# Combining expert outputs on three engines: blocks handed from VectorE to ScalarE and TensorE, and the kept tail from GpSimd to them

## The chip, the cores and the metric

The kernel runs on one core of a Trainium2 chip. The metric is device time in microseconds (us) of one execution; lower is better. A core has four engines that compute, each with its own in-order instruction queue: TensorE (PE, matrix products into PSUM), VectorE (DVE), ScalarE (ACT) and GpSimd (POOL); SyncE (SP) issues most transfers. They meet only through semaphores. PSUM has eight banks of 128 x 512 words.

## What is computed

Two layers over 8192 nodes of width 128. The first is a graph convolution over 32 graphs. The second, which the change touches, is a mixture of four experts whose gates come from an attention layer over 524,288 edges:

```python
agg = segment_sum(h[src] * alpha, dst) + b_gat
scores = layernorm(agg).reshape(M, HEADS, NUM_EXPERTS).mean(1)
topk_s, topk_i = top_k(scores, 2);  w = softmax(topk_s)
for ei in range(4):
    g = where(topk_i == ei, w, 0).sum(-1)
    out = out + g[..., None] * (gelu(x @ W1[ei] + b1[ei]) @ W2[ei] + b2[ei])
x = x + out
```

Everything is fp32; `out` is one sum per node of four gated expert outputs and the residual `x`.

## The kernel before

The nodes are 64 tiles of 128 (`xs[:, t, :]`), two tiles to a group. The expert outputs of all nodes (512 words per node) are computed early, before the gates are known. Those of 24 groups (48 tiles) are stored to HBM and those of the last 8 groups (16 tiles, `eo_kept`) stay on the chip. A **block** is two groups, four tiles; there are 12 stored blocks, 0 to 11, and four kept ones.

The end of the kernel, from about 885 us, goes in four **parts** of 16 tiles, `g` = 0 to 3. Before it, and beside it, GpSimd gathers one table row per edge list entry with 384 indirect transfers (L554), 96 for each part; part `g` can begin when `rows_in[g]` is complete. In each part:

- ScalarE regroups the gathered rows (L950), TensorE transposes them (L784), VectorE computes attention weights (`weights`, L1438 to L1450), which TensorE transposes back (L789) and ScalarE puts in place (L942).
- VectorE multiplies (`values`, L1457); ScalarE and VectorE split the rows into three bf16 pieces (L932, L1464, L937, L1469).
- TensorE sums over the edges, 48 products into four banks of `ps_H`, then 48 into four banks of `ps_four` (L797). VectorE empties each half (`take_bank`, L1478). ScalarE moves half of the result across partitions by a transfer (L963), and TensorE and ScalarE prepare the marks of the next part (`mark`, L773 and L924 to L927).
- VectorE merges and computes the gates (`merge`, `gating`, L1487 to L1561) with one Exp on ScalarE in between (L970).

`combine(b)` (L1577) adds the four gated expert outputs of block `b` to `xs` on VectorE, 16 instructions of 128 x 128. A block is loaded from HBM by SP (L462, 1 MB) into one of four slots, which come free when the slot's earlier block is combined (`SLOT_OF`), and stored by SP when `combined` says so (L487). The order on VectorE is written by hand: the blocks of a part's nodes are combined during the next part, two before `take_bank` and two after it; in part 3 two of them stand before `weights` instead. So blocks 0 to 3 fall in part 1, blocks 4 to 7 in part 2 and blocks 8 to 11 in part 3, together with the kernel's last gates.

After the last gates come the 16 kept tiles: VectorE combines eight of them as above, ScalarE scales the other eight (L976), and GpSimd adds their four pieces and the residual (L592, L594, L596). SP stores them, and the kernel ends.

Of the kernel before, what the change touches and what calls it, by code (L numbers as in the profile page):

```python
# [24 lines left out]
GRAPHS, NODES, D = 32, 256, 128  # L25
# [10 lines left out]
OWN = M // P  # L36
# [28 lines left out]
PART_BLOCKS = BLOCKS // (PARTS - 1)  # L65
SLOT_OF = (0, 1, 0, 1, 0, 1, 2, 0, 1, 2, 3, 0)
KEPT_BLOCKS = 2

def build(nc, x, adj, eps, W1, b1, rms_w, W2, b2, W_gat, att_src, att_dst, b_gat, ln_g, ln_b,  # L70
# [4 lines left out]
    with ctx:  # L75
# [44 lines left out]
        def region(at):  # L120

            def take(shape, dt=fp32):
# [9 lines left out]
                if len(shape) > 1:  # L132
# [173 lines left out]
        sums = [ps_H[:, :, :, :].rearrange("p a b n -> p (a b n)").rearrange("p (g w) -> p g w", g=4), ps_four[:, :, :]]  # L306
# [17 lines left out]
                 "combined", "others_combined", "sum_chain", "gated", "iota_done", "zero_done"]  # L324
# [63 lines left out]

        def part_tiles(m, g):

            return m[:, g * PART_TILES:(g + 1) * PART_TILES]

        others = [(eo_kept[:, t, :], TILES - PAIR * KEPT + t) for t in range(KEPT_BLOCKS * BLOCK_TILES, PAIR * KEPT)]
# [4 lines left out]
        def _(sp):  # L398
# [100 lines left out]
            for b in range(KEPT_BLOCKS):  # L499
                sp.wait_ge(s["combined"], BLOCKS + b + 1)  # L500
                rstore(GROUPS - KEPT + BLOCK * b, BLOCK, out_stored[1])
            for b in range(KEPT // BLOCK - KEPT_BLOCKS):
                sp.wait_ge(s["others_combined"], BLOCK_TILES * (b + 1))
                rstore(GROUPS - KEPT + BLOCK * (KEPT_BLOCKS + b), BLOCK, out_stored[0])
            sp.wait_ge(out_stored[0], 16 * (KEPT // BLOCK - KEPT_BLOCKS))
            sp.wait_ge(out_stored[1], 16 * (BLOCKS + KEPT_BLOCKS))
# [5 lines left out]
        def _(pool):  # L512
# [73 lines left out]

            pool.wait_ge(s["gates_ready"], PARTS)
            for n, (of, t) in enumerate(others):
                row = xs[:, t, :]  # L590
                pool.wait_ge(s["gated"], n + 1)
                pool.tensor_tensor(of[:, 0:2 * D], of[:, 0:2 * D], of[:, 2 * D:4 * D], ALU.add).then_inc(s["sum_chain"], 1)  # L592
                pool.wait_ge(s["sum_chain"], 2 * n + 1)
                pool.tensor_tensor(of[:, 0:D], of[:, 0:D], of[:, D:2 * D], ALU.add).then_inc(s["sum_chain"], 1)  # L594
                pool.wait_ge(s["sum_chain"], 2 * n + 2)
                pool.tensor_tensor(row, row, of[:, 0:D], ALU.add).then_inc(s["others_combined"], 1)  # L596

        @block.tensor
        def _(pe):
# [167 lines left out]
            def mark(g):  # L767

                if g:
                    pe.wait_ge(s["agg_out"], 2 * g - 1)  # L770
                    pe.wait_ge(s["marks_ready"], g)
                for k, m in enumerate((self_, empty)):
                    last = nc.tensor.matmul(halfH[2 + k][:, 0:OWNED], chosen[:, g, :], m, start=True, stop=True)  # L773
                last.then_inc(s["marks_in_psum"], 1)

            pe.wait_ge(s["marks_made"], 1)
            mark(0)
            for g in range(PARTS):
                if g:
                    pe.wait_ge(s["agg_out"], 2 * g)  # L780
                for k in range(2):
# [3 lines left out]
                    last.then_inc(s["terms_in_psum"], 1)  # L785
                for k, ready in ((1, "back_ready"), (0, "exp_done")):
# [14 lines left out]
                if g + 1 < PARTS:  # L801
                    mark(g + 1)

        @block.scalar
        def _(act):
# [114 lines left out]
            def mark(g):  # L920
# [3 lines left out]
                nc.scalar.activation(marks[:, 0, 0:OWNED], halfH[2][:, 0:OWNED], ACT.Identity)  # L924
                nc.scalar.activation(marks[:, 1, 0:OWNED], halfH[2][:, 0:OWNED], ACT.Identity, bias=ones[:, 0:1], scale=-1.0)
# [706 lines left out]
```

## Time and profile before

| what | value |
|---|---|
| time, median of 3 runs | 1152.58 us (1148.36 to 1153.88) |
| the profiled execution | 1152.78 us, its span 1151.0 us |
| VectorE busy | 905.2 us, 79% of the span |
| TensorE busy, mean granted clock | 802.5 us, 0.769 of full speed |
| ScalarE, GpSimd busy | 440.0 us, 611.7 us |
| the stage that the change touches | about 885 us to the end |

How to read it: all rows come from one profiled execution, in microseconds from the start of its span.
### The profile page before, as it was taken

The numbers are of one execution on the slowest core, as the hardware profiler recorded it, in microseconds if no ns is written. First come the engines' busy times: TensorE is split into PE (matmuls) and PEld (weight loads), VectorE is DVE, ScalarE is ACT, GpSimd is POOL, SyncE is SP. The second block draws the span as 40 slices with busy tenths as digits, with TensorE's granted clock in tenths as the row PEclk, the third lists the DMA queues.
The fourth block names the chain that finished last, engine by engine and source line by source line (L and its number), as shares of the span: only waits on it lengthen the run. The fifth ranks groups of instructions, "written<-read, shape, count | busy, mean of one in ns | idle before, by whom it ended". The sixth has DMA issues, their size and how long they took to land. (4 is left out here: it accounts for less than half of the span.)

```text
span 1151.0 us, 17715 instructions
## 1 busy us (share of the span) xinstructions
PE 802.5 (70%) x5180; PEld 688.4 (60%) x5180; DVE 905.2 (79%) x3070; ACT 440.0 (38%) x1069; POOL 611.7 (53%) x553
## 2 busy tenths in 40 slices
PE   0004888989999988969999999999996415041130
PEld 0003777878888977848888888888884404040030
DVE  7999787867888877997999501888887578989877
ACT  1008788884455544525555553000001212120303
POOL 2000000006777760077777777888887778888004
PEclk9999888888999988979999999555555555555555
DMA  8000011112222112112222300000000012425001
GB/s 251 2 0 28 24 32 43 31 44 48 56 48 63 30 9 27 74 47 65 83 65 83 100 10 9 7 6 7 6 7 9 10 49 82 156 59 178 19 22 37
DMA packets 73043, 55.45 MB, mean 48 GB/s; under 512 B 32534, under 2 KB 65689, under 8 KB 72988
## 3 DMA queue, kind: packets, MB, share of 16 engines
q1 hardware_dynamic: 56140, 48.72, 13.4%
q0 software_dynamic: 16384, 5.54, 5.3%
q10 hardware_dynamic: 464, 0.59, 0.2%
q8 instruction: 19, 0.31, 0.1%
q14 instruction: 36, 0.29, 0.1%
HBM read 36.65 MB, written 17.76 MB: 47 GB/s over the span
## 5 line engine op out<-in xcount | busy, mean ns | idle before, releaser
L554 POOL DMA_INDIRECT sb_arena<-table,sb_arena x384 | 463.7, 1208 | 169.5 <-issue 116.7
L538 POOL DMA_INDIRECT sb_late<-lists,sb_window_at x128 | 127.9, 999 | 297.6 <-DMA lists<-sb_arena 255.9
L729 PE MATMUL ps_four<-sb_late 128*128 128x64 bf16 x1232 | 159.8, 301 | 3.7 <-DVE sb_late L1307 0.3
L1305 DVE TENSOR_TENSOR sb_late<-sb_far_lo,sb_iota_lo 128x1792 bf16<-128x1792 bf16 x88 | 96.1, 1092 | 84.0 <-PE ps_four L729 81.0
L729 PEld LDWEIGHTS ps_four<-sb_late 128*128 128x128 bf16 x1232 | 141.8, 143 | 21.5 <-DVE sb_late L1307 18.3
L702 PE MATMUL ps_four<-sb_we,sb_arena 128*128 128x128 f32 x1024 | 131.9, 282 | 0.0
L702 PEld LDWEIGHTS ps_four<-sb_we,sb_arena 128*128 128x128 f32 x1024 | 119.7, 192 | 14.7 <-issue 14.7
L694 PE MATMUL ps_H<-sb_x2nT,sb_we 128*128 (+1 forms) x512 | 124.7, 388 | 0.0
L887 ACT ACTIVATE sb_arena<-ps_H,sb_be_c 128x256 f32<-128x256 f32 x256 | 107.0, 470 | 30.7 <-PE ps_H L694 28.7
L694 PEld LDWEIGHTS ps_H<-sb_x2nT,sb_we 128*128 128x128 f32 x512 | 95.2, 196 | 11.0
L820 ACT ACTIVATE sb_arena<-sb_arena,sb_owner_mid 128x368 f32<-128x368 f32 x128 | 76.8, 600 | 53.4 <-DVE sb_arena L1048 49.8
L636 PE MATMUL ps_four<-sb_arena 128*128 128x256 f32 x128 | 37.0, 415 | 73.4 <-DVE sb_var L1162 73.4
L628 PE MATMUL ps_H<-sb_arena,sb_w 128*128 128x256 f32 x256 | 82.9, 481 | 0.2 <-DVE sb_arena L1229 0.2
L671 PE MATMUL ps_four<-sb_ones,sb_arena 128*128 128x1 f32 x512 | 65.9, 258 | 16.3 <-ACT sb_arena L838 16.3
L671 PEld LDWEIGHTS ps_four<-sb_ones,sb_arena 128*128 128x128 f32 x512 | 66.0, 209 | 18.1 <-ACT sb_arena L833 18.1
L636 PEld LDWEIGHTS ps_four<-sb_arena 128*128 128x128 f32 x128 | 27.5, 221 | 80.3 <-DVE sb_arena L1216 74.1
L1229 DVE SCALAR_TENSOR_TENSOR sb_arena<-ps_H,sb_b_c,sb_arena 128x256 f32<-128x256 f32 x128 | 53.1, 477 | 23.8 <-ACT sb_arena L843 23.2
L647 PE MATMUL ps_four<-sb_w,sb_arena 128*128 128x128 f32 x512 | 69.0, 291 | 0.0
L854 ACT ACTIVATE sb_arena<-sb_arena,sb_rms_c 128x256 f32<-128x256 f32 x128 | 54.6, 497 | 37.4 <-DVE sb_arena L1229 37.4
L924 ACT ACT_TABLE_LOAD x1 | 1.3, 1283 | 170.6 <-PE ps_H L773 170.6
L628 PEld LDWEIGHTS ps_H<-sb_arena,sb_w 128*128 128x128 f32 x256 | 59.1, 242 | 10.1 <-issue 0.5
L647 PEld LDWEIGHTS ps_four<-sb_w,sb_arena 128*128 128x128 f32 x512 | 62.7, 200 | 3.9 <-issue 0.2
(247 smaller groups left out, 1422.5 us busy)
## 6 DMA issues: line engine op xcount, KB each, us to landing
outputs<-sb_arena SPq DMA_DIRECT2D x24, 512.0 KB, 2.7
sb_arena<-outputs SPq DMA_DIRECT2D x12, 1024.0 KB, 6.3
sb_arena<-in_adj SPq DMA_DIRECT2D x32, 256.0 KB
sb_arena<-table,sb_arena POOLq DMA_INDIRECT x384, 2.8
sb_x2nT<-in_L_ffn_edge_index SPq DMA_DIRECT2D x8, 512.0 KB, 7.6
sb_xs<-in_x SPq DMA_DIRECT2D x32, 128.0 KB, 2.2
out_x<-sb_xs SPq DMA_DIRECT2D x16, 256.0 KB, 2.6
sb_late<-lists,sb_window_at POOLq DMA_INDIRECT x128
```

The source lines that it names most:

```text
L538: pool.indirect_dma_start(bk.bitcast(i32)[:, p * WINDOW:(p + 1) * WINDOW], None, lists, bass.IndirectOffsetOnAxis(ap=window_at[:, p:p + 1] ...
L554: pool.indirect_dma_start(rows[:, g, c, o, :], None, table[0:M, :], bass.IndirectOffsetOnAxis(ap=idxT[:, at:at + 1], axis=0), bounds_check ...
L628: last = nc.tensor.matmul(ps_H[:, q, c, :], w1[:, c * P:(c + 1) * P], aggT[:, q, :], start=True, stop=True)
L636: last = nc.tensor.matmul(ps_A, xn[:, p, mt, :], adjT[:, p, mt, :], start=(mt == 0), stop=(mt == 1))
L647: last = nc.tensor.matmul(ps_O[:, nt, :], ss[:, q, c, nt * P:(nt + 1) * P], w2[:, c, :], start=False, stop=(nt == 1 and c == HC - 1))
L671: last = nc.tensor.matmul(ps_Q[:, u:u + 1], sq[:, q, c, u * P:(u + 1) * P], ones[:, 0:1], start=(c == 0), stop=(c == HC - 1))
L694: last = nc.tensor.matmul(halfH[e][:, c * GROUP:(c + 1) * GROUP], we1[:, e, c * P:(c + 1) * P], x2nT[:, bass.ds(g * GROUP, GROUP)], start= ...
L702: last = nc.tensor.matmul(obank[k][:, (j // 2) * D:(j // 2 + 1) * D], hh[1 - p][:, j, k * P:(k + 1) * P], we2[:, j, :], start=False, stop= ...
L729: last = nc.tensor.matmul(ps_F, hot_lo[k][:, :, c], hot_hi[k][:, :, c], start=(first and c == 0), stop=(end and c == FB - 1))
L820: nc.scalar.activation(sign_out, owner, ACT.Sign, bias=owner_mid[:, o:o + 1], scale=2.0, accum_out=above[:, o:o + 1]).then_inc(s["above_co ...
L887: last = nc.scalar.activation(hh[p][:, 2 * e + c, :], halfH[e][:, c * GROUP:(c + 1) * GROUP], ACT.Gelu, bias=be1_c[:, 2 * e + c:2 * e + c ...
L1305: V.tensor_tensor(hot_lo[k], far_lo[:, bass.ds(b * FB, FB)].unsqueeze(1).to_broadcast([P, P, FB]), iota_lo[:, :, :], ALU.is_equal)
```

## The change

- **Between parts.** Of the 12 stored blocks six (2, 3, 6, 7, 8, 9: `SUMMED`) leave VectorE's `combine`. For each of them ScalarE multiplies the 16 pieces by their gates in place (`scale_block`), TensorE adds the four experts of the block's four tiles by four products with the identity into one bank (`block_sum`), and VectorE adds that bank to `xs` in one instruction (`add_sum`). Blocks 0, 1, 4, 5, 10 and 11 stay on VectorE, now one before the two `take_bank` and one after. Blocks 8 and 9 move from VectorE to this path, ahead of `weights` of part 3, and so does block 7, which stood in part 2.
- **Banks.** The edge sums use three banks of each half in place of four, with six batches to a bank, so that two banks are free for `block_sum`; `take_bank` reads each half with four instructions in place of two. The marks move to other banks, so that `mark` waits for both halves to be emptied, where it waited for one.
- **The end.** VectorE combines ten kept tiles in place of eight. For the other six ScalarE scales, TensorE adds the four pieces and the residual into a bank, and ScalarE copies the sum to `xs`. GpSimd has no work there. The kept tiles are stored by eight transfers of one group in place of four of two.

The diff at its core:

```diff
+PER_BANK = 6
-KEPT_BLOCKS = 2
+KEPT_TILES = 10
-        sums = [ps_H[:, :, :, :].rearrange("p a b n -> p (a b n)").rearrange("p (g w) -> p g w", g=4), ps_four[:, :, :]]
+        sums = [ps_H[:, :, :, :].rearrange("p a b n -> p (a b n)").rearrange("p (g w) -> p g w", g=4)[:, 0:3, :], ps_four[:, 0:3, :]]
+        marks_bank = [halfH[2], bank_O[:, :]]
+        block_bank = [bank_S[:, :], halfH[3]]
+        SUMMED = (2, 3, 6, 7, 8, 9)
...
 @block.gpsimd
-            for n, (of, t) in enumerate(others):
-                pool.tensor_tensor(of[:, 0:2 * D], of[:, 0:2 * D], of[:, 2 * D:4 * D], ALU.add)
-                pool.tensor_tensor(of[:, 0:D], of[:, 0:D], of[:, D:2 * D], ALU.add)
-                pool.tensor_tensor(row, row, of[:, 0:D], ALU.add)
...
 @block.tensor
             def mark(g):
-                    pe.wait_ge(s["agg_out"], 2 * g - 1)
+                    pe.wait_ge(s["agg_out"], 2 * g)
+            def block_sum(b):
+                pe.wait_ge(s["scaled"], SUMMED.index(b) + 1)
+                some(pe, s["combined"], b - 1, None)
+                of = eo_back[SLOT_OF[b]]
+                for e in range(EXPERTS):
+                    last = nc.tensor.matmul(block_bank[b % 2], ident[:, :], of[:, :, e * D:(e + 1) * D],
+                                            start=(e == 0), stop=(e == EXPERTS - 1))
+                last.then_inc(s["block_in_psum"], 1)
             for g in range(PARTS):
+                if g == PARTS - 1:
+                    for b in (block_of(g - 1, 3), block_of(g, 0), block_of(g, 1)):
+                        block_sum(b)
...
+                if g == 2:
+                    block_sum(block_of(g - 1, 3))
...
+                if g in (1, 2):
+                    block_sum(block_of(g, 2))
+            for n, (of, t) in enumerate(others):
+                pe.wait_ge(s["gated"], n + 1)
+                for e in range(EXPERTS):
+                    nc.tensor.matmul(others_bank[n], ident[:, :], of[:, e * D:(e + 1) * D], start=(e == 0), stop=False)
+                nc.tensor.matmul(others_bank[n], ident[:, :], xs[:, t, :], start=False, stop=True)
...
 @block.scalar
+            def scale_block(b):
+                act.wait_ge(s["gates_ready"], b // PART_BLOCKS + 1)
+                act.wait_ge(eo_loaded[SLOT_OF[b]], 16 * turns(b))
+                for u in range(BLOCK_TILES):
+                    for e in range(EXPERTS):
+                        last = nc.scalar.activation(of, of, ACT.Identity, scale=gates[:, b * BLOCK_TILES + u, e:e + 1])
+                last.then_inc(s["scaled"], 1)
             for g in range(PARTS):
+                if g == PARTS - 1:
+                    for b in (block_of(g - 1, 3), block_of(g, 0), block_of(g, 1)):
+                        scale_block(b)
+                by_heads(g)
+                if g == 2:
+                    scale_block(block_of(g - 1, 3))
...
+                if g in (1, 2):
+                    scale_block(block_of(g, 2))
+            gate(0)
+            gate(1)
+            for n in range(2, len(others)):
+                gate(n)
+                keep_sum(n - 2)
...
 @block.vector
+            def add_sum(b):
+                dve.wait_ge(s["block_in_psum"], SUMMED.index(b) + 1)
+                V.tensor_tensor(to, to, block_bank[b % 2].rearrange("p (t d) -> p t d", t=BLOCK_TILES), ALU.add)
             for g in range(PARTS):
                 if g == PARTS - 1:
-                    combine(before.pop(0))
-                    combine(before.pop(0))
+                    for b in (block_of(g - 1, 3), block_of(g, 0), block_of(g, 1)):
+                        add_sum(b)
...
-                for b in before[:len(before) // 2]:
-                    combine(b)
+                if g == 2:
+                    add_sum(block_of(g - 1, 3))
+                if g:
+                    combine(block_of(g, 0 if g < PARTS - 1 else 2))
                 take_bank(2 * g)
                 take_bank(2 * g + 1)
-                for b in before[len(before) // 2:]:
-                    combine(b)
+                if g:
+                    combine(block_of(g, 1 if g < PARTS - 1 else 3))
                 merge(g)
                 gating(g)
+                if g in (1, 2):
+                    add_sum(block_of(g, 2))
-            for b in range(KEPT_BLOCKS):
-                combine(BLOCKS + b)
+            combine_kept(0, 4)
+            combine_kept(4, 4)
+            combine_kept(8, KEPT_TILES - 8)
```

Here `block_of(g, k)` is block `4 (g - 1) + k`. The order of the instructions shows it at two engines. The first place is ScalarE between the merge of part 2 and the Exp of part 3's weights; before, with `rows_in3` the gathers of part 3:

```order
L967 ACTIVATE sb_late<-sb_late 128x16x4 [waits merge_in]
L968 ACTIVATE sb_far_e<-sb_far_e 128x64
L970 ACTIVATE sb_gates<-sb_sc 128x64 [waits gates_e]
L950 ACTIVATE sb_iota_lo<-sb_arena 128x384 [waits terms_in_psum,rows_in3]
L950 ACTIVATE sb_iota_lo<-sb_arena 128x384 [waits terms_in_psum]
L953 ACTIVATE sb_arena<-sb_arena 128x384 [waits exp_in]
```

and after, where L976 is the scaling of a block, L984 the regrouping and L1015 the gates' Exp (`eo_loaded2` is the load into slot 2):

```order
L1011 ACTIVATE sb_far_e<-sb_far_e 128x64
L976 ACTIVATE sb_arena<-sb_arena,sb_gates 128x128 [waits eo_loaded2,gates_ready]
L976 ACTIVATE sb_arena<-sb_arena,sb_gates 128x128 x15
L1015 ACTIVATE sb_gates<-sb_sc 128x64 [waits gates_e]
L976 ACTIVATE sb_arena<-sb_arena,sb_gates 128x128 [waits eo_loaded0,gates_ready]
L976 ACTIVATE sb_arena<-sb_arena,sb_gates 128x128 x15
L976 ACTIVATE sb_arena<-sb_arena,sb_gates 128x128 [waits eo_loaded1,gates_ready]
L976 ACTIVATE sb_arena<-sb_arena,sb_gates 128x128 x15
L976 ACTIVATE sb_arena<-sb_arena,sb_gates 128x128 [waits eo_loaded2,gates_ready]
L976 ACTIVATE sb_arena<-sb_arena,sb_gates 128x128 x15
L984 ACTIVATE sb_iota_lo<-sb_arena 128x384 [waits terms_in_psum,rows_in3]
```

Four scalings moved in, of blocks 6, 7, 8 and 9, and three of them stand ahead of the regrouping of part 3. The second place is TensorE between the edge sums of part 2 and the first transposes of part 3; before:

```order
L797 MATMUL ps_four<-sb_late,sb_arena 64x72 x47
L773 MATMUL ps_H<-sb_arena,sb_epsI 128x384 [waits marks_ready,agg_out]
L773 MATMUL ps_H<-sb_arena,sb_epsI 128x384
L784 MATMUL ps_H<-sb_ident,sb_iota_lo 128x128 [waits by_head_ready,agg_out]
L784 MATMUL ps_H<-sb_ident,sb_iota_lo 128x128 x2
```

and after, where L782 is `block_sum` and L797 the transposes of the terms:

```order
L773 MATMUL ps_H<-sb_arena,sb_epsI 128x384 [waits marks_ready,agg_out]
L773 MATMUL ps_four<-sb_arena,sb_epsI 128x384
L782 MATMUL ps_four<-sb_arena,sb_ident 128x512 [waits combined,scaled]
L782 MATMUL ps_four<-sb_arena,sb_ident 128x512 x3
L782 MATMUL ps_H<-sb_arena,sb_ident 128x512 [waits combined,scaled]
L782 MATMUL ps_H<-sb_arena,sb_ident 128x512 x3
L782 MATMUL ps_four<-sb_arena,sb_ident 128x512 [waits combined,scaled]
L782 MATMUL ps_four<-sb_arena,sb_ident 128x512 x3
L782 MATMUL ps_H<-sb_arena,sb_ident 128x512 [waits combined,scaled]
L782 MATMUL ps_H<-sb_arena,sb_ident 128x512 x3
L797 MATMUL ps_H<-sb_ident,sb_iota_lo 128x128 [waits by_head_ready,agg_out]
```

Four sums of four products each moved in, and the transposes of part 3 now stand behind them.

## Rows read from the trace of the kernel before

**Rows 1.** The page: busy time of the engines, granted clock in 40 slices.

```profile
PE 802.5 (70%) x5180; PEld 688.4 (60%) x5180; DVE 905.2 (79%) x3070; ACT 440.0 (38%) x1069; POOL 611.7 (53%) x553
PEclk9999888888999988979999999555555555555555
```

**Rows 2.** Chain that ended last: start us, us, what.

```profile
1127.02 15.47 DVE sb_xs L1577 x29
```

**Rows 3.** Timeline of VectorE, part 0, which combines no block.

```profile
906.65 2.64 DVE L1469 TENSOR_TENSOR sb_late<-sb_arena,sb_late 128x1152 bf16<-128x1152 f32 x2
914.14 1.42 DVE L1478 TENSOR_REDUCE sb_late<-ps_H 64x192 f32<-64x576 f32 x2 [4.86 <-PE ps_H L797]
919.90 1.41 DVE L1478 TENSOR_REDUCE sb_late<-ps_four 64x192 f32<-64x576 f32 x2 [4.34 <-PE ps_four L797]
925.56 0.23 DVE L1487 TENSOR_TENSOR sb_a_dst<-sb_late,sb_far_e 128x64 f32<-128x64 f32 x1 [4.25 <-DMA sb_late<-sb_late]
```

**Rows 4.** Timeline of VectorE, part 1: first block combined, start of the merge.

```profile
965.23 8.48 DVE L1577 SCALAR_TENSOR_TENSOR sb_xs<-sb_arena,sb_gates,sb_xs 128x128 f32<-128x128 f32 x32
...
986.26 0.22 DVE L1487 TENSOR_TENSOR sb_a_dst<-sb_late,sb_far_e 128x64 f32<-128x64 f32 x1
```

**Rows 5.** Timeline of VectorE, part 2, then two blocks and the weights of part 3.

```profile
1025.81 8.48 DVE L1577 SCALAR_TENSOR_TENSOR sb_xs<-sb_arena,sb_gates,sb_xs 128x128 f32<-128x128 f32 x32
...
1046.24 0.21 DVE L1487 TENSOR_TENSOR sb_a_dst<-sb_late,sb_far_e 128x64 f32<-128x64 f32 x1
...
1066.67 8.48 DVE L1577 SCALAR_TENSOR_TENSOR sb_xs<-sb_arena,sb_gates,sb_xs 128x128 f32<-128x128 f32 x32
1075.07 0.54 DVE L1438 TENSOR_TENSOR sb_arena<-ps_H,sb_arena 128x384 f32<-128x384 f32 x1
```

**Rows 6.** Timeline of ScalarE: gates' Exp of parts 1 and 2, regrouping, kept scaling.

```profile
1001.72 0.26 ACT L970 ACTIVATE sb_gates<-sb_sc 128x64 f32<-128x64 f32 x1 [14.41 <-DVE sb_sc L1556]
...
1061.70 0.26 ACT L970 ACTIVATE sb_gates<-sb_sc 128x64 f32<-128x64 f32 x1 [14.42 <-DVE sb_sc L1556]
1068.13 2.21 ACT L950 ACTIVATE sb_iota_lo<-sb_arena 128x384 f32<-128x384 f32 x2 [6.17 <-DMA sb_arena<-table,sb_arena]
...
1127.02 9.45 ACT L976 ACTIVATE sb_x2nT<-sb_x2nT,sb_gates 128x128 f32<-128x128 f32 x32 [1.09 <-DVE sb_gates L1561]
```

**Rows 7.** Timeline of TensorE: transposes back, marks, transposes of the terms.

```profile
1014.37 1.54 PE L789 MATMUL ps_four<-sb_ident,sb_arena 128*128 128x128 f32 x6 [9.34 <-DVE sb_arena L1450]
...
1036.40 2.93 PE L773 MATMUL ps_H<-sb_arena,sb_epsI 128*128 128x384 f32 x4
1069.44 1.86 PE L784 MATMUL ps_H<-sb_ident,sb_iota_lo 128*128 128x128 f32 x6 [30.11 <-ACT sb_iota_lo L950]
```

**Rows 8.** Stretches: us, busy PE, PEld, DVE, ACT, POOL, granted clock, DMA share, GB/s.

```profile
1025.00:1035.00 10.00, 10.00 (x86) 10.00 (x85) 10.00 (x35) 0.00 (x0) 8.78 (x5) 0.50 0.45 132
...
1040.00:1041.00 1.00, 0.00 (x0) 0.00 (x0) 1.00 (x6) 1.00 (x3) 1.00 (x1) 1.00 0.69 189
```

**Rows 9.** The page, groups of TensorE at the high clock: count | busy us, mean ns.

```profile
L702 PE MATMUL ps_four<-sb_we,sb_arena 128*128 128x128 f32 x1024 | 131.9, 282 | 0.0
L694 PE MATMUL ps_H<-sb_x2nT,sb_we 128*128 (+1 forms) x512 | 124.7, 388 | 0.0
```

**Rows 10.** Stretches of the end, all engines, columns as in rows 8.

```profile
1127.00:1128.40 1.40, 0.00 (x0) 0.00 (x0) 1.38 (x6) 1.38 (x5) 0.00 (x0) 0.50 0.00 0
1128.50:1136.50 8.00, 0.00 (x0) 0.00 (x0) 8.00 (x14) 7.97 (x28) 7.31 (x13) 0.50 0.09 28
1136.50:1142.90 6.40, 0.00 (x0) 0.00 (x0) 6.40 (x12) 0.00 (x0) 5.81 (x11) 0.50 0.03 8
```

**Rows 11.** Line 487, the stores of `out_x`: duration ns, first and last start.

```profile
L487 SPq DMA_DIRECT2D out_x<-sb_xs x16: 380/386/551, 969.5 to 1144.5; - x16
```

**Rows 12.** Line 1438, a 128 x 384 add from PSUM: duration ns min/median/max.

```profile
L1438 DVE TENSOR_TENSOR sb_arena<-ps_H,sb_arena x4: 543/547/557, 889.5 to 1075.1; 128x384 f32<-128x384 f32 x4
```

**Rows 13.** Line 462, the block loads of 1 MB, issue to landing.

```profile
DMA to landing us min/median/max: 5.0/6.3/9.5
```

More of the change, by code:

```diff
@@ L1473, in take_bank @@
                 dve.wait_ge(s["agg_in_psum"], k + 1)
-                by_part = sums[k % 2][0:OWN, :, 0:4 * 3 * ROW].rearrange("p g (t u s v) -> p g t u s v", u=2, s=3, v=ROW)
-                tiles_ = slice(BATCH // 2 * (k % 2), BATCH // 2 * (k % 2 + 1))
-                outs = [m[k // 2 % 2][0:OWN, tiles_, :].rearrange("p (g t) v -> p g t v", g=4) for m in (agg, odd)]
-                for u, o in enumerate(outs):
-                    last = V.reduce_sum(o, by_part[:, :, :, u, :, :].rearrange("p g t s v -> p g t v s"), AX.X)
+                for first, past, each in ((0, 2, PER_BANK), (2, 3, BATCH - 2 * PER_BANK)):
+                    by_bank = sums[k % 2][0:OWN, first:past, 0:each * 3 * ROW].rearrange("p g (t u s v) -> p g t u s v", u=2, s=3, v=ROW)
+                    at = BATCH // 2 * (k % 2) + first * PER_BANK // 2
+                    for u, m in enumerate((agg, odd)):
+                        o = m[k // 2 % 2][0:OWN, at:at + (past - first) * each // 2, :].rearrange("p (g t) v -> p g t v", g=past - first)
+                        last = V.reduce_sum(o, by_bank[:, :, :, u, :, :].rearrange("p g t s v -> p g t v s"), AX.X)
                 last.then_inc(s["agg_out"], 1)
@@ L1581, in combine @@
                 last.then_inc(s["combined"], 1)
+                gated_n[0] += (EXPERTS - 1) * BLOCK_TILES
             for g in range(PARTS):
-                before = [PART_BLOCKS * (g - 1) + b for b in range(PART_BLOCKS)] if g else []
                 hots_of(2 * g)
@@ L1595, in _, with combine_kept @@
                 lowest(2 * g + 1)
[L1596 to L1597 removed]
+                if g == 2:
+                    add_sum(block_of(g - 1, 3))
+                if g:
+                    combine(block_of(g, 0 if g < PARTS - 1 else 2))
                 take_bank(2 * g)
                 take_bank(2 * g + 1)
[L1600 to L1601 removed]
+                if g:
+                    combine(block_of(g, 1 if g < PARTS - 1 else 3))
                 merge(g)
                 gating(g)
[L1604 to L1605 removed]
+                if g in (1, 2):
+                    add_sum(block_of(g, 2))
+            def combine_kept(first, n):
+                base = gated_n[0] + (EXPERTS - 1) * first
+                for e in range(EXPERTS):
+                    for u in range(n):
+                        row = xs[:, TILES - PAIR * KEPT + first + u, :]
+                        if e:
+                            dve.wait_ge(s["comb_chain"], base + (e - 1) * n + u + 1)
+                        last = V.scalar_tensor_tensor(row, eo_kept[:, first + u, e * D:(e + 1) * D],
+                                                      gates[:, TILES - PAIR * KEPT + first + u, e:e + 1], row, ALU.mult, ALU.add)
+                        if e < EXPERTS - 1:
+                            last.then_inc(s["comb_chain"], 1)
+                        elif u % PAIR:
+                            last.then_inc(s["combined"], 1)
+            combine_kept(0, 4)
+            combine_kept(4, 4)
+            combine_kept(8, KEPT_TILES - 8)
 _INS = ["x", "adj", "L0_gnn_epsilon", "L0_gnn_W1", "L0_gnn_b1", "L0_gnn_rms_weight", "L0_gnn_W2", "L0_gnn_b2",
```

74 lines of the change are left out of this document (40 added, 34 removed).

## The prediction

> **What bounds the kernel now.** I read the page first. VectorE has the largest busy share, 79%, but TensorE is at 70% and its clock is at the low level in the whole last part of the span [rows 1], so an average decides nothing and the end has to be read as a stage of its own. The chain that ended last gives its final piece: VectorE combining kept tiles from 1127.02 on [rows 2]. From there I went back along VectorE's timeline.
>
> In part 0, which has no block to combine, VectorE waits three times between its last remainder (906.65 + 2.64 = 909.3) and the merge at 925.56: 4.86 and 4.34 us for the two halves of the edge sums and 4.25 us for a transfer, 16.3 us in all [rows 3]. In parts 1 and 2 it combines four blocks there. A block costs 8.48 / 2 = 4.24 us, so four cost 17.0 us, and the same stretch takes 986.26 - 965.23 = 21.0 us and 1046.24 - 1025.81 = 20.4 us [rows 4, 5]. So of 17.0 us of combining only 4 to 5 us stand on the path; the rest fills waits that part 0 shows empty. VectorE bounds parts 1 and 2, by little.
>
> Part 3 has a second bound. Its regrouping on ScalarE began at 1068.13, after 6.17 us of waiting for the gathers [rows 6], and the transposes at 1069.44 for 1.86 us [rows 7], so the terms were there at 1071.3; VectorE reached the weights at 1075.07, after two blocks [rows 5]. A lead that VectorE wins in parts 1 and 2 is worth at most 1075.1 - 1071.3 = 3.8 us if the gathers stay where they are.
>
> In the tail the same combining runs at half speed. Six instructions ran in the first 1.38 us, beside ScalarE alone: 0.23 to 0.27 us each. Beside GpSimd there were 14 in 8.00 us and, with ScalarE done, 12 in 6.40 us: 0.53 to 0.57 each [rows 10]. So GpSimd's adds slow it, not ScalarE.
>
> **The change, part by part.** The sum is made against the profiled execution, 1152.78 us, whose span is 1151.0 us with 1.8 us around it; that is 0.2 us above the median of the runs shown, 1152.58.
>
> *Emptying the edge sums.* Four instructions in place of two move the same words. Two more starts cost between 0 and 0.4 us: an instruction over 576 words takes 1.42 / 2 = 0.71 us [rows 3], one over 384 takes 0.55 [rows 12], so the fixed part is at most about 0.2. I take +0.2 us per half. The first half's share lies beside TensorE's second half (5.8 us from one to the other, 919.90 - 914.14); the second's is on the path, in each of four parts.
>
> *The marks* now wait for both halves. They are needed only before the merge's Exp, and the 2.93 us of TensorE [rows 7] and four short copies lie beside the transfer's 4.25 us [rows 3]. I cost them at nothing; without that cover it would be up to 0.5 us in each of three parts.
>
> *Parts 1 and 2 on VectorE.* One block (4.24) goes into the first wait (4.86) and one into the transfer's (4.25), so the stretch falls to part 0's 16.3 + 0.2 = 16.5 us. Part 1 wins 21.0 - 16.5 = 4.5. Each `add_sum` adds 512 words from PSUM: by the 0.55 us for 384, 0.7 us [rows 12]. Block 2's is added after part 1's gates, +0.7. Block 3's stands before a combine in part 2: 0.7 + 4.24 = 4.9 against the wait of 4.86, so +0.1; part 2 wins 20.4 - 16.6 = 3.8. With +0.2 from part 0 the Exp of part 2's gates ends 0.2 - 4.5 + 0.7 - 3.8 = -7.4 us earlier, at 1061.96 - 7.4 = 1054.6 [rows 6].
>
> *What a block costs TensorE.* Four products of 512 columns, eight matrix instructions. Low clock: six transposes of 128 columns take 1.54 us [rows 7], about 0.22 each, so eight of 512 cost 8 x 4 x 0.22 = 7.2 us; the marks' four of 384 columns in 2.93 us give 7.8 at most. I take 7.3. High clock: 512 instructions of 256 columns in 124.7 us are 0.244 each [rows 9], so eight of 512 cost at most 3.9 us. Which one? The clock stood at 0.50 through ten us of edge sums that kept TensorE busy all the time, and was at 1.00 in the microsecond after the marks' four fp32 products [rows 7, 8]. A block's sum is eight such fp32 instructions, so I let it rise inside the first sum of a row: 5.6 us, the middle of 3.9 and 7.3, and 3.9 for those that follow at once.
>
> *Block 3's sum* stands between two transposes that part 2 needs. It can start 2.2 us (regrouping) plus one scaling after the gates' Exp of part 1. A scaling is 16 instructions: 9.45 / 32 x 16 = 4.7 us [rows 6]. So it runs from 6.9 to 12.5 us after the Exp (14.2 at the low clock). The transposes back wait for VectorE until 1014.37 - 1001.98 = 12.4 us after it [rows 6, 7], 13.1 with block 2's add. Cost 0, bound +1.1. Blocks 2 and 6 are scaled and summed beside `gating` (ScalarE waits 14.4 us there [rows 6]); they cost nothing.
>
> *Part 3 up to the weights.* Three scalings now stand ahead of the regrouping on ScalarE's queue: 1054.6 + 0.1 + 3 x 4.7 = 1068.8. The load for block 9 needs slot 2, free only when block 6 is added: gates at 1054.6 + 1.1 [rows 6], the add at 1056.4, a store and the load issued by 1057.3, landed 5.0 to 9.5, median 6.3 us later [rows 13]: 1063.6, in time for its scaling at 1064.1, at worst 2.7 us late. TensorE sums block 7 from 1059.4 to 1065.0, block 8 to 1068.9, block 9 to 1072.8. Behind that wait the transposes of part 3, and on VectorE the three adds ahead of the weights. VectorE starts the weights at 1072.8 + 0.7 and a step, 1073.6. Before: 1075.07. That is -1.5 us, and VectorE's lead of 7.4 us is spent waiting. The gathers, even unchanged at 1068.1, are no longer last.
>
> *Part 3 after the weights* is as before, +0.2 for the second half.
>
> *The tail.* VectorE: 40 instructions at 0.265 are 10.6 us. The path over TensorE: the first tile scaled at 1.3 us, ten instructions a tile, 0.22 each low, 131.9 / 1024 = 0.129 each high [rows 9]. Two tiles low (to 5.7) and four high (1.3 each) end at 10.9, the copy and steps at 11.6. All low: 1.3 + 6 x 2.2 + 0.5 = 15.0; all high it is ScalarE's 24 scalings and six copies, about 9 to 11. SP then issues the last VectorE store and three more, 0.39 us each [rows 11] and 0.45 with the step between: the last begins at 10.6 + 3 x 0.45 + 0.1 = 12.1 us after the gates. Before, it began at 1144.5 - 1127.0 = 17.5 [rows 11]. That is -5.4 us, bounds -6 and -2.4. What follows the last store I leave as it was.
>
> Sum: -1.5 + 0.2 - 5.4 = -6.7, so 1152.78 - 6.7 = **1146.1 us**.
>
> **A page on the clock.** The Trainium skill, TensorE: Matmul & The Clock Gate (HAM oscillation), says that a TensorE left waiting falls to half rate and that each burst after a wait starts there. This speaks against the change, which puts short bursts into waits. By it alone blocks 2, 3, 6, 7 and the tail begin low, as I have them; if none of them rose again, the result would be the first rival's. The trace agrees on the fall: 0.50 in most of the end, and 1.00 only for some microseconds after the marks [rows 1, 8].
>
> **Rivals.** (1) *TensorE becomes the bound.* The clock stays at 0.50. Three sums then cost 3 x 7.3 = 21.9 from 1059.4: 1081.3, the weights at 1082.1, +7.0; the tail -2.4 at best: 1152.8 + 7.0 + 0.2 - 2.4 = 1157.6, slower than before. It decides from 5.0 us a sum (1059.4 + 3 x 5.0 + 0.8 = 1075.2). For it: 0.50 in every slice of the end [rows 1]. Against: the rise after the marks. (2) *Only the tail's products stay low*, after 15 us in which TensorE has nothing to do: -1.5 + 0.2 - 2.4 = -3.7, 1149.1. (3) *The load of block 9 is late* by 2.7: 1148.8. For it: it is issued beside the last gathers and a store; against: the median. (4) *The change does not free VectorE*: the kept tiles run slowly for another reason. Then 40 x 0.53 = 21.2 us, the tail +5.1, 1156.6. Rows 10 speak against it. (5) *VectorE's lead arrives*, if ScalarE and TensorE are done sooner than their rows say: the weights at 1071.3, -3.8 in place of -1.5: 1143.8.
>
> **How the numbers follow.** Forecast 0.62; rivals 0.10, 0.12, 0.07, 0.03 and 0.06. The forecast's own range is 1143.5 to 1149.5: costs of +1.7 (block 7 wholly low), +1.1 (block 3) and 1.5 (marks) one way, less than my 3.9 and 0.2 the other, and executions of before that differ by 5.5 us. Half a percent, 5.8 us, is about what a measurement of this kernel can tell from no change; faster means below 1146.8, slower above 1158.3. A little over half of the forecast, and rival 5, are below: 0.44. Slower: half of rival 1, some of 4 and what I have not seen: 0.10. The rest, 0.46, lies between. The range 1142.5 to 1154 leaves out rivals 1 and 4 and little else.
>
> **What would show it.** Right: the weights of part 3 released by TensorE and not by a combine, at 1073 to 1075; the granted clock at 1.00 during the sums of blocks 8 and 9; the kept combines at 0.265 us each; no idle time over 1 us at `add_sum` of block 3. Wrong: sums of 7 us each, a scaling of block 9 that waits for its load, or a last store more than 13 us after the gates.

## The result: 0.9913 of the time before, and the profile after

The changed kernel took 1141.27 us, median of 6 runs (1136.81 to 1142.21), beside 1149.96 us (6 runs) for the kernel before; the ratio is 0.9913, 95% interval 0.989 to 0.9937. A second comparison on one chip (the first run of the experiments) gave 0.9888, 0.9872 to 0.9904. The profiled execution took 1141.60 us with a span of 1139.9 us, 11.1 us less than the span before. The prediction had 6.7 us less, 1146.1, with 1142.5 as the low end of its range: the direction is right, and for the profiled execution the forecast gain is 4.5 us too small. In medians the gain is 8.7 us (12.2 in the second comparison). The forecast started from an execution of 1152.78 us, 2.8 us above the median of the six, so a part of the distance to its range is scatter of the kernel before.

To see where the 11.1 us are, the span is best cut at two instructions that stand in both kernels: VectorE's reciprocal in the gating of part 0 and in that of part 3. They are shown for the kernel before, then for the kernel after (timeline of VectorE: start us, duration us, what).

```profile
941.89 0.25 DVE L1560 RECIPROCAL sb_gs<-sb_gs 128x16 f32<-128x16 f32 x1
...
1126.47 0.25 DVE L1560 RECIPROCAL sb_gs<-sb_gs 128x16 f32<-128x16 f32 x1
```

```profile
942.83 0.25 DVE L1619 RECIPROCAL sb_gs<-sb_gs 128x16 f32<-128x16 f32 x1
...
1124.84 0.25 DVE L1619 RECIPROCAL sb_gs<-sb_gs 128x16 f32<-128x16 f32 x1
```

| kernel | to part 0 | parts 0 to 3 | part 3 to the end | span |
|---|---|---|---|---|
| before | 941.9 | 184.6 | 24.5 | 1151.0 |
| after | 942.8 | 182.0 | 15.1 | 1139.9 |
| changed again | 943.8 | 182.8 | 15.0 | 1141.6 |
| one late GpSimd add | 942.6 | 182.7 | 20.0 | 1145.3 |
| the same add, early | 939.4 | 182.8 | 15.2 | 1137.4 |
| stores in pairs | 942.5 | 182.6 | 15.1 | 1140.2 |
| new end alone | 939.5 | 184.6 | 15.0 | 1139.1 |
| new work between parts alone | 943.0 | 182.5 | 24.6 | 1150.1 |
| regrouping first | 941.4 | 171.4 | 15.0 | 1127.8 |
| three blocks on VectorE | 943.7 | 179.2 | 15.0 | 1137.9 |
| one-hot rows early | 941.8 | 174.6 | 15.1 | 1131.4 |

The first column is nearly the same work in all of them and still differs by 4.4 us from run to run; the six times of the changed kernel differ by 5.4. The other two repeat within 0.8 and 0.2 us wherever the code is the same. So the gain is 1.8 to 2.6 us between the parts and 9.5 us behind the last gates.

**Between the parts** VectorE's timeline answers to [rows 3 to 5]. These rows are parts 1 and 2 of after; the bracket is the idle time ahead and what ended it.

```profile
966.17 4.28 DVE L1641 SCALAR_TENSOR_TENSOR sb_xs<-sb_arena,sb_gates,sb_xs 128x128 f32<-128x128 f32 x16
971.10 1.54 DVE L1537 TENSOR_REDUCE sb_late<-ps_H 64x144 f32<-64x432 f32 x4 [0.66 <-PE ps_H L812]
976.86 1.54 DVE L1537 TENSOR_REDUCE sb_late<-ps_four 64x144 f32<-64x432 f32 x4 [4.22 <-PE ps_four L812]
978.33 4.27 DVE L1641 SCALAR_TENSOR_TENSOR sb_xs<-sb_arena,sb_gates,sb_xs 128x128 f32<-128x128 f32 x16
...
1039.08 0.23 DVE L1546 TENSOR_TENSOR sb_a_dst<-sb_late,sb_far_e 128x64 f32<-128x64 f32 x1 [0.27 <-DMA sb_late<-sb_late]
```

One block fills the wait for the first half of the edge sums to 0.66 us, the other that for the transfer to 0.27 us or nothing. The wait for the second half, 4.22 us, stays empty. In part 3 the three adds come ahead of the weights:

```profile
1065.83 0.69 DVE L1627 TENSOR_TENSOR sb_xs<-sb_xs,ps_H 128x512 f32<-128x512 f32 x1 [5.70 <-PE ps_H L782]
1069.27 0.69 DVE L1627 TENSOR_TENSOR sb_xs<-sb_xs,ps_four 128x512 f32<-128x512 f32 x1 [2.75 <-PE ps_four L782]
1072.70 0.69 DVE L1627 TENSOR_TENSOR sb_xs<-sb_xs,ps_H 128x512 f32<-128x512 f32 x1 [2.75 <-PE ps_H L782]
1073.31 0.55 DVE L1496 TENSOR_TENSOR sb_arena<-ps_H,sb_arena 128x384 f32<-128x384 f32 x1
```

VectorE stands idle for 5.70 + 2.75 + 2.75 = 11.2 us and then starts the weights, 1.8 us sooner than the kernel before [rows 5]. What it waits for is on TensorE, and TensorE's first sum on ScalarE:

```profile
1054.65 14.11 ACT L976 ACTIVATE sb_arena<-sb_arena,sb_gates 128x128 f32<-128x128 f32 x48
1068.67 2.19 ACT L984 ACTIVATE sb_iota_lo<-sb_arena 128x384 f32<-128x384 f32 x2
```

```profile
1059.47 6.33 PE L782 MATMUL ps_H<-sb_arena,sb_ident 128*128 128x512 f32 x8 [9.51 <-ACT sb_arena L976]
1065.63 3.60 PE L782 MATMUL ps_four<-sb_arena,sb_ident 128*128 128x512 f32 x8
1069.07 3.60 PE L782 MATMUL ps_H<-sb_arena,sb_ident 128*128 128x512 f32 x8
1072.50 0.82 PE L797 MATMUL ps_H<-sb_ident,sb_iota_lo 128*128 128x128 f32 x6
```

The clock of these sums is in the stretches (columns as in [rows 8]): 0.50 at the start of block 7's sum, after 9.5 us of waiting, and full from block 8's on.

```profile
1059.50:1062.50 3.00, 3.00 (x4) 1.45 (x5) 0.63 (x2) 3.00 (x11) 0.00 (x0) 0.50 0.68 261
1062.50:1065.50 3.00, 3.00 (x5) 1.11 (x5) 0.00 (x0) 3.00 (x12) 0.00 (x0) 0.62 0.00 0
1065.70:1072.40 6.70, 6.70 (x17) 2.92 (x16) 1.37 (x2) 5.16 (x13) 0.00 (x0) 1.00 0.74 239
```

**At the end** 40 combines of kept tiles start at 1125.38 and take 10.59 us, 0.265 each; beside GpSimd they took 0.53 to 0.57 [rows 10]. The last store starts at 1137.5, 12.1 us after the gates; before it was 17.5 [rows 11]. That is 5.4 us. The timeline of VectorE, then the stores' line as in [rows 11]:

```profile
1125.38 10.59 DVE L1681 SCALAR_TENSOR_TENSOR sb_xs<-sb_x2nT,sb_gates,sb_xs 128x128 f32<-128x128 f32 x40
```

```profile
L498 SPq DMA_DIRECT2D out_x<-sb_xs x20: 380/386/513, 970.5 to 1137.5; - x20
```

The rest lies behind the last store, in the closing instructions of the program's end. GpSimd's last add in the kernel before, then line 75 of that kernel (engine's queue, operation, count: duration ns min/median/max, start us), then line 76 of after:

```profile
1142.42 0.45 POOL L596 TENSOR_TENSOR sb_xs<-sb_xs,sb_x2nT 128x128 f32<-128x128 f32 x1
```

```profile
L75 POOLq DRAIN  x1: 8424/8424/8424, 1142.4 to 1142.4; - x1
L75 SPq COMPARE_BRANCH  x1: 38/38/38, 1147.8 to 1147.8; - x1
L75 SPq EVENT_SEMAPHORE  x1: 17/17/17, 1151.0 to 1151.0; - x1
```

```profile
L76 POOLq DRAIN  x1: 26904/26904/26904, 1035.6 to 1035.6; - x1
L76 SPq COMPARE_BRANCH  x1: 38/38/38, 1139.5 to 1139.5; - x1
L76 SPq EVENT_SEMAPHORE  x1: 17/17/17, 1139.8 to 1139.8; - x1
```

SyncE's branch stands behind its wait for the last store. Before, it came at 1147.8, and nothing closed until GpSimd's drain was over at 1142.4 + 8.4 = 1150.8, 8.0 us after the end of its last add (1142.42 + 0.45). After, the drain stands in GpSimd's queue from 1035.6 and is over at 1062.5, 7.9 us after the end of its last gather instruction:

```profile
1053.64 1.00 POOL L565 DMA_INDIRECT sb_arena<-table,sb_arena  x1 [0.30 <-issue]
```

With that long past, the span closes 0.4 us after SyncE. Behind the last store there were 6.5 us before and 2.4 after: 3.2 against 0.4 from SyncE's branch on, and 3.3 against 2.0 from the store to the branch.

### The profile page after: what moved, and what is told of

The parts are those of the page before. It is cut to its first block and busy times, and to the rows that moved or that the text cites. A ratio compares the mean times of both kernels' runs of the same rounds, so it can differ in the third digit from the quotient of the medians.

```text
span 1139.9 us, 17951 instructions
## 1 busy us (share of the span) xinstructions
PE 840.0 (74%) x5288; PEld 708.7 (62%) x5288; DVE 879.0 (77%) x3004; ACT 466.9 (41%) x1163; POOL 585.8 (51%) x529
## 5 line engine op out<-in xcount | busy, mean ns | idle before, releaser
L565 POOL DMA_INDIRECT sb_arena<-table,sb_arena x384 | 451.0, 1174 | 169.5 <-issue 116.7
L671 PEld LDWEIGHTS ps_four<-sb_ones,sb_arena 128*128 128x128 f32 x512 | 66.5, 210 | 17.5 <-ACT sb_arena L857 17.4
```

The costliest lines, as they stand in the source:

```text
L565: pool.indirect_dma_start(rows[:, g, c, o, :], None, table[0:M, :], bass.IndirectOffsetOnAxis(ap=idxT[:, at:at + 1], axis=0), bounds_check ...
L671: last = nc.tensor.matmul(ps_Q[:, u:u + 1], sq[:, q, c, u * P:(u + 1) * P], ones[:, 0:1], start=(c == 0), stop=(c == HC - 1))
```

## Experiments

The theory: the mechanisms of the prediction hold and GpSimd's drain is the part that it missed. The first rival: the smaller stores (128 KB in place of 256) give the gain at the end. The second: it lies between the parts. Four kernels went on one chip first.

**The changed kernel again.**

> The changed kernel as it is, on the same chip as the three kernels below, as their base. Profiled span near 1139.9 us, last store starting near 1137.6, GpSimd's closing drain over long before. All theories expect the same here.

Measured: 1140.75 us, ratio 0.9888 (0.9872 to 0.9904). The span is 1141.6, 1.7 above the expectation, 1.8 us of it lying ahead of part 3's gates; behind them it is 15.0 us, as in the first profile (15.1).

**One late GpSimd add.**

```
+            pool.wait_ge(s["others_in_psum"], len(others))
+            pool.tensor_tensor(masked[:, 0, :], ident[:, :], ident[:, :], ALU.add)
```

> One GpSimd add of 128x128 on scratch is put behind TensorE's last sum (about 1134.4 us); nothing waits for it. Theory (GpSimd's closing drain, which lasted 8.4 us in the kernel before, held its end): the add ends near 1135.0, the drain about 8.0 later near 1143.0, the span near 1143.3, 3.4 us longer than the changed kernel's; SyncE is past its waits near 1139.5 as without it. Rival (the gain at the end came from the smaller stores): span 1139.9, no change. Rival (any GpSimd instruction costs its own length): +0.5 at most.

Measured: 1145.66 us, ratio 0.9935 (0.9918 to 0.9952), 4.9 us above the changed kernel on the same chip. Its timeline of GpSimd and its closing instructions:

```profile
1136.72 0.40 POOL L599 TENSOR_TENSOR sb_late<-sb_ident 128x128 f32<-128x128 f32 x1 [82.17 <-PE ps_H L829]
```

```profile
L76 POOLq DRAIN  x1: 8361/8361/8361, 1136.7 to 1136.7; - x1
L76 SPq COMPARE_BRANCH  x1: 38/38/38, 1140.0 to 1140.0; - x1
```

An add of 0.40 us whose result nobody reads costs 4.9 us. SyncE is done when it was, and the span (1145.3) closes 0.2 us after the drain (1136.7 + 8.4 = 1145.1). The size is above the expected 3.4 because TensorE's last sum, and so the add, came 2.3 us later than I had put it.

**The same add at the gates.**

```
+            pool.wait_ge(s["gates_ready"], PARTS)
+            pool.tensor_tensor(masked[:, 0, :], ident[:, :], ident[:, :], ALU.add)
```

> The same GpSimd add, but as soon as the last part's gates are there (about 1125.4 us). Theory (drain): the drain ends near 1134, 5 us before the last store has landed, so the span stays at 1139.9 within 0.4. Rival (a GpSimd instruction anywhere near the end costs): near 1143, as the late one. Rival (the stores): 1139.9.

Measured: 1140.18 us, ratio 0.9885 (0.9863 to 0.9907), as the changed kernel.

```profile
L76 POOLq DRAIN  x1: 8517/8517/8517, 1122.8 to 1122.8; - x1
L76 SPq COMPARE_BRANCH  x1: 37/37/37, 1137.0 to 1137.0; - x1
```

The drain is as long (8.5 us), ends at 1131.3, before the last store, and costs nothing: 15.2 us from the gates to the end. So it is not the instruction that costs but how late it is: in both the drain is over 7.9 us after the end of the add. The rival of the smaller stores said no change for both adds; the late one refutes it as the whole cause.

**Stores of 256 KB.**

```
-            for g in range(KEPT_TILES // PAIR):
+            for g, n in ((0, 2), (2, 2), (4, 1)):
...
-            for g in range(KEPT - KEPT_TILES // PAIR):
+            for g, n in ((0, 1), (1, 2)):
```

> The kept tiles are stored in transfers of 256 KB (two groups) where there are two, so that the last one is of 256 KB, as in the kernel before. Theory (drain for most of it, store size for the rest): the last store starts where it did and lands 1.0 us later (2.9 against 1.9 us), span near 1140.9, +1.0. Rival (store size is the whole gain at the end): +4.2, span near 1144.

Measured: 1141.28 us, ratio 0.9899 (0.9882 to 0.9915), no change; 15.1 us behind the gates. Part of my expectation was wrong: five stores in place of eight leave SyncE sooner (its last issue ends 12.1 us after the start of the kept combines, in place of 12.6), and the larger one lands about 0.4 later, so nothing is left. Storing in fewer, larger pieces costs nothing in the end. What differs in the kernel before is how much is stored at the very end. Its last three stores, of 256 KB each, were issued within 1.5 us:

```profile
1143.57 0.93 SPq L487 DMA_DIRECT2D out_x<-sb_xs  x2
...
1144.00 1.10 SPq L487 DMA_DIRECT2D out_x<-sb_xs  x2
```

(two stretches of the timeline that overlap in the store at 1144.00). From the start of the last store to SyncE's branch it took 3.3 us there. In this run the last three stores hold 0.52 MB in place of 0.79, issued within 1.4 us, and it took 2.4; in the changed kernel 0.39 MB within 1.6 us, and 2.0. I read the 1.3 us as that volume; no run put all of it back with the rest of the new end, so smaller stores stay a possible cause of this part.

**The two halves of the change, each alone**, in a second comparison on one chip. The new end with the work between the parts of before:

```
-KEPT_BLOCKS = 2
+KEPT_TILES = 10
...
+                nc.tensor.matmul(others_bank[n], ident[:, :], xs[:, t, :], start=False, stop=True).then_inc(s["others_in_psum"], 1)
...
-                pool.tensor_tensor(row, row, of[:, 0:D], ALU.add).then_inc(s["others_combined"], 1)
```

> The kernel before with the new end alone (VectorE ten kept tiles, ScalarE and TensorE six, no GpSimd); the work between parts is as before. Theory (the end is worth 24.0 - 14.5 us from the last part's gates to the end of the span, the work between parts 1.6): gates near 1127.0, span 1141.5, 9.5 less than before, ratio 0.992. Rival (the gain lies between the parts, the end only uncovers it): ratio above 0.996.

Measured: 1140.31 us, ratio 0.9897 (0.9869 to 0.9926). Parts 0 to 3 take 184.6 us, as before, and the end 15.0, as after; that the span is 2.4 below the expectation lies ahead of part 0's gates (939.5 against 941.9).

The changed work between the parts with the end of before (the same hunks the other way round):

> The changed work between parts with the old end (VectorE eight kept tiles, ScalarE eight, GpSimd adds them). Theory: gates near 1125.4, the span 24.0 later near 1149.4, 1.6 less than before (ratio 0.9986); GpSimd's last add ends some 16 us after the gates, and its closing drain about 8.0 us later is the last thing in the span, 3 us after SyncE has passed its waits. Rival (the gain lies between the parts): ratio under 0.995. Rival (the drain is not what holds the end): the drain ends before SyncE's last wait.

Measured: 1150.83 us, ratio 0.9968 (0.9946 to 0.9989). Parts 0 to 3 take 182.5, the end 24.6, and the drain holds it again:

```profile
L76 POOLq DRAIN  x1: 8424/8424/8424, 1141.4 to 1141.4; - x1
L76 SPq COMPARE_BRANCH  x1: 38/38/38, 1146.8 to 1146.8; - x1
```

1141.4 + 8.4 = 1149.8 of 1150.1. The two halves add up to the whole change (9.5 and 2.1 us of the cut spans), and the rival that puts the gain between the parts falls: its ratios were above 0.996 for the first kernel and under 0.995 for the second. (The second interval just reaches 0.995; the cut spans decide.)

**Regrouping first.** If the 11.2 us that VectorE waits in part 3 are the price of the order, another order has them back. ScalarE scales one block only ahead of the regrouping, TensorE transposes ahead of its sums, and VectorE starts the weights at once. Block 9 goes back to VectorE, so that block 10 falls into the empty wait for the second half.

```
-        SUMMED = (2, 3, 6, 7, 8, 9)
+        SUMMED = (2, 3, 6, 7, 8)
...
                 if g == PARTS - 1:
-                    for b in (block_of(g - 1, 3), block_of(g, 0), block_of(g, 1)):
-                        scale_block(b)
+                    scale_block(block_of(g - 1, 3))
                 by_heads(g)
...
+                if g == PARTS - 1:
+                    scale_block(block_of(g, 0))
...
                 take_bank(2 * g)
+                if g == PARTS - 1:
+                    combine(block_of(g, 2))
                 take_bank(2 * g + 1)
```

> The changed kernel, but in the last part ScalarE regroups the gathered rows behind one scaled block instead of three, TensorE transposes them ahead of its block sums, VectorE starts the weights at once, adds the two sums in later waits and takes the third block itself while it waits for the second bank. Theory (the 11.2 us that VectorE waits for three block sums are the price of the order; the gathers have landed by 1059.4): weights start near 1062.6 instead of 1073.3, gates near 1114.9, span near 1129.4, 10.5 under the changed kernel's; if the gathers land as late as 1062.5, weights near 1065.7 and span 1132.5. Rival (the gathers bind, as in the kernel before, where they were regrouped at 1068.1): weights near 1071, span near 1137.5. Rival (TensorE's block sums at the low clock, 6.3 us each, now delay the transposes back and the bank sums): 3 to 6 us of the gain are given back, span 1133 to 1136.

Measured: 1128.91 us (1125.73 to 1131.34), ratio 0.9788 (0.9762 to 0.9815): the fastest kernel of all, some 12 us under the changed one. Timelines of ScalarE, then of TensorE, then of VectorE:

```profile
1058.87 2.19 ACT L983 ACTIVATE sb_iota_lo<-sb_arena 128x384 f32<-128x384 f32 x2
```

```profile
1060.16 1.86 PE L794 MATMUL ps_H<-sb_ident,sb_iota_lo 128*128 128x128 f32 x6 [9.74 <-ACT sb_iota_lo L983]
1061.81 5.87 PE L782 MATMUL ps_H<-sb_arena,sb_ident 128*128 128x512 f32 x8
```

```profile
1061.17 0.56 DVE L1496 TENSOR_TENSOR sb_arena<-ps_H,sb_arena 128x384 f32<-128x384 f32 x1 [1.48 <-PE ps_H L794]
```

The regrouping follows the scaling without a wait, so the gathers had landed by 1058.9, and the weights start at 1061.17, 12.1 us sooner than in after; expected were 1062.6. Neither rival came: the gathers do not bind at 1068, where the kernel before still waited for them [rows 6], and block 7's sum, at 0.50 until 1066, ends at 1067.7, before VectorE adds it at 1069.14. Parts 0 to 3 are 171.4 us against 182.0 to 182.8. From the start of the weights to the reciprocal of part 3 it takes 51.6 us against 51.5, so the whole gain lies ahead of the weights; handing block 9 back was not tried without the new order.

**Three blocks on VectorE in the middle parts too**, which takes two of the five sums away (the cut is shown against the kernel with the regrouping first).

```
-        SUMMED = (2, 3, 6, 7, 8)
+        SUMMED = (3, 7, 8)
...
-                if g == PARTS - 1:
-                    combine(block_of(g, 2))
+                if g:
+                    combine(block_of(g, 1 if g < PARTS - 1 else 2))
```

> The same, and in the two middle parts VectorE combines a third block itself, while it waits for the second bank (4.22 us), so that two of the five block sums go. Theory (the 4.28 us of a block fit this wait, and the two adds of 0.69 us go): span 1.4 under that of the kernel with the regrouping moved, near 1128.0. Rival (the third block of the first of these parts, loaded only when the first one is done, has not landed): VectorE waits up to 2 us for it there, span 0.6 above.

Measured: 1137.86 us, ratio 0.9864 (0.9837 to 0.9891), 9 us slower than the last one; 7.8 us of it lie between the gates of parts 0 and 3. Theory and rival both missed. From gates to gates part 1 takes 58.1 us (56.0 with the regrouping alone) and part 2 takes 63.2 (57.5): the worst waits are in part 2, not in part 1.

```profile
1035.00 4.29 DVE L1637 SCALAR_TENSOR_TENSOR sb_xs<-sb_arena,sb_gates,sb_xs 128x128 f32<-128x128 f32 x16 [2.90 <-DMA sb_arena<-outputs]
1040.67 4.27 DVE L1637 SCALAR_TENSOR_TENSOR sb_xs<-sb_arena,sb_gates,sb_xs 128x128 f32<-128x128 f32 x16
1048.52 0.23 DVE L1542 TENSOR_TENSOR sb_a_dst<-sb_late,sb_far_e 128x64 f32<-128x64 f32 x1 [3.58 <-DMA sb_late<-sb_late]
```

Block 5 is combined one wait sooner and its load has not landed (2.90 us), and behind that the transfer of the odd rows is late (3.58, against 0.98 with the order of the last kernel).

**One-hot rows early.** The same wait filled without a third block: VectorE's second block between the two halves, the next part's one-hot rows in the transfer's wait (the cut is shown against the changed kernel).

```
-                hots_of(2 * g)
-                hots_of(2 * g + 1)
...
+                if g:
+                    combine(block_of(g, 1 if g < PARTS - 1 else 2))
                 take_bank(2 * g + 1)
+                if g < PARTS - 1:
+                    hots_of(2 * g + 2)
+                    hots_of(2 * g + 3)
+                else:
+                    combine(block_of(g, 3))
```

> The kernel with the regrouping moved, and besides in every part VectorE's second block goes into the wait for the second bank (4.22 us) and the one-hot rows of the next part (3.69 us) into the wait for the transfer of the odd rows (4.3 to 4.5 us); loads are as they were. From part to part VectorE gains 3.6 to 3.7 us, so the third part's gates come some 10.5 us sooner after those of part 0 (102.9 instead of 113.4). Theory (the gathers of the last part now bind: the last one is issued near 1053 and lands some 2.9 us later): ScalarE waits for them, the weights of part 3 start near 1059.3 instead of 1061.2, span near 1126.0, 1.9 less. Rival (VectorE binds to the end): the gain of three parts arrives, span near 1117. Rival (earlier loads and sums collide with the odd rows' transfer, as with the third block on VectorE): gain under 5 us in the parts, span 1128 or above.

Measured (another chip): 1133.09 us, ratio 0.9837 (0.9819 to 0.9854), slower than with the regrouping alone. The theory's gathers do not bind; in part 2 the rival of the collisions does:

```profile
1029.29 4.29 DVE L1641 SCALAR_TENSOR_TENSOR sb_xs<-sb_arena,sb_gates,sb_xs 128x128 f32<-128x128 f32 x16 [2.48 <-DMA sb_arena<-outputs]
1034.95 3.68 DVE L1482 TENSOR_TENSOR sb_arena<-sb_arena,sb_w 128x1024 bf16<-128x1024 bf16 x6
1042.17 0.23 DVE L1546 TENSOR_TENSOR sb_a_dst<-sb_late,sb_far_e 128x64 f32<-128x64 f32 x1 [3.54 <-DMA sb_late<-sb_late]
```

From the gates of part 1 to those of part 2 it takes 61.2 us in place of 57.5. A block that is combined sooner also lets the next load of 1 MB start sooner: here at 1034.08, one us ahead of the odd rows' transfer at 1035.05, which then lands after 7.1 us. With the regrouping alone that load started at 1037.93, behind the transfer's issue at 1033.25, which landed after 5.1 us. In part 1, which gained 0.5 us of the expected 3.6, it is the same: the transfer lands after 5.7 us with a load issued 1.1 us ahead (5.9 with three blocks on VectorE), 2.1 and 2.3 us in the changed kernel and with the regrouping alone, where the load ahead had landed. That the load is what holds it is read from these starts and was not tried by itself.

Part 3 gains nothing (57.9 us from gates to gates in both), for another reason. VectorE is free for the weights sooner, but waits for TensorE's transposes:

```profile
1064.71 0.56 DVE L1496 TENSOR_TENSOR sb_arena<-ps_H,sb_arena 128x384 f32<-128x384 f32 x1 [5.09 <-PE ps_H L794]
```

The wait was 1.48 us with the regrouping alone. The scaling of block 7, 4.76 us from 1057.75, still stands ahead of the regrouping on ScalarE, so that queue now takes the 3.6 us that VectorE won.

## Why the prediction was wrong

The step that failed is one sentence of the tail: "What follows the last store I leave as it was." It was put at nothing without a row, and it held 4.1 of the 4.4 us that the profiled span fell beyond the forecast. 2.8 of them are GpSimd's drain: that a late drain holds the end is shown by the late and the early add and by the old end put back, and the size is read from the closing instructions. 1.3 are the last stores, which were read and not tried. The line was there to be read: after each kernel's last store the closing instructions stand in the trace, and the prediction took GpSimd out of the last stage without asking when that engine is done. The view of waits hides it. For SyncE in the kernel before (who waited, on whom: us in total, times, longest) it says:

```profile
SPq L75 <- PEq L75: 3.1, 1, 3.1
SPq L75 <- DMA out_x<-sb_xs: 1.8, 1, 1.8
```

The 3.1 us are there, but put down to TensorE's queue, whose own drain was over at 1104.9:

```profile
L75 PEldq DRAIN  x1: 2382/2382/2382, 1102.5 to 1102.5; - x1
```

The ceiling of 3.8 us on VectorE's lead was wrong too, though the forecast did not come to rest on it. It held "if the gathers stay where they are", and they moved. From the reciprocal of part 0 to the start of the last gather it takes 117.7 and 123.0 us in the two kernels with the old work between the parts, and 110.4 to 110.8 in the six profiles of the changed work. Why GpSimd is done sooner was not tried.

The other steps held. (Of part 0's 16.3 us, which the prediction calls waits, 13.45 are waits and the rest is work; the sum uses them as a stretch and is not touched.)

- Emptying the edge sums: four instructions take 1.54 us for 1.41, +0.13 (predicted +0.2).
- Parts 1 and 2: from gates to gates 60.6 and 60.0 before, 56.0 and 56.5 after, so 4.7 and 3.5 us won (57.2 to 57.5 and so 2.5 to 2.8 in the repeats; predicted 4.5, and 3.8 less the add's 0.7); the add takes 0.69. Part 0's wait was the right measure.
- The sums: 6.33, 3.60 and 3.60 us, 13.2 from the first start to the last end (predicted 5.6, 3.9, 3.9, so 13.4). The Trainium skill, TensorE: Matmul & The Clock Gate (HAM oscillation), says that a burst behind a wait starts at half rate; the trace agrees, with 0.50 for the first 3 us of block 7's sum. That it rises inside the sum was the open question: it does, and rival 1 falls.
- Block 3's sum: 6.22 us, done when the transposes back were asked for; cost 0, as taken.
- Part 3: the regrouping at 1068.67 (1068.8), the weights at 1073.3 (1073.6), behind adds that waited for TensorE. Rival 3 did not come: the 48 scalings ran without a gap. Rival 5 did not come either, but the regrouping kernel shows what it pointed at: the gathers had landed by 1058.9, and the weights could start 12 us sooner by another order of the queues (with block 9 back on VectorE), without a faster ScalarE or TensorE.
- The tail: 40 combines in 10.59 us (10.6), the last store 12.1 us after the gates (12.1). Rival 4 falls with the 0.265 us per combine; rival 2 because the clock rises within the second tile (0.50 from 1126.8 to 1129.5, 0.99 from there to 1134.5), or the third in the repeated run, whose end is as early.

So the gates of part 3 came 1.6 us sooner (forecast 1.3) and the last store another 5.4 us (forecast 5.4); the omitted term of -4.1 carried the profiled time to 1141.6, past the range's low end. That the 1.6 is so near 1.3 is in part luck: it is the gain of 2.6 us between the gates of parts 0 and 3 (forecast 1.5; 1.8 to 2.1 in the repeats), less 0.9 us by which part 0's gates came later in this execution.

## What to carry to other kernels

In this kernel GpSimd counted until its closing drain was over, not until its last result was used. When a change removes or adds an engine's work near the end, read each engine's closing instructions behind the last store, and give the engine whose drain is over last its work early. Cut the span at instructions that both kernels have before comparing; here that separates 4 us of scatter from stretches that repeat within 0.2 and 0.8 us. Where an engine waits for work that others queue for it, look first at the order of those queues: moving the regrouping ahead of two scaled blocks, and the adds behind the weights, with one block handed back to VectorE, brought some five times what the change itself brought between the parts.

## What the runs showed of the hardware

- GpSimd's closing drain is over 7.9 to 8.0 us after the end of its last instruction in all eleven profiles, whether that is an add of 0.40 to 0.56 us or a gather of 1.0 to 1.3. Its listed length (8.4 to 29.7 us) says little: in the changed kernel it is listed from 1035.6, 19.0 us before the last gather was over. VectorE's drain lasted 0.5 to 1.6 us, ScalarE's 0.3 to 3.5, TensorE's 1.6 to 2.4.
- The transfer of the odd rows, issued by ScalarE one us behind SyncE's issue of a load of 1 MB, landed after 7.1 us (one-hot rows early) and 7.7 us (three blocks on VectorE) in place of 5.1 in part 2, and after 5.7 and 5.9 us in place of 2.1 to 2.3 in part 1.
